# A fused attention and mixture-of-experts layer: accumulator rows load ahead of the last scatter, and the last stage works in five groups

## What is computed

```python
x = x + _layernorm(_L0_attn_ref(_layernorm(x), Wq, Wk, Wv, Wo))   # 16 heads of 16, causal, rotary
x = x + _layernorm(_L0_ffn_ref(_layernorm(x), gate_w, ...))
# _L0_ffn_ref: 16 experts (inner size 176), the 4 best of each row, and a shared expert (704)
combine = (one_hot(topk_idx, E) * topk_w[..., None]).sum(1)
shared = _silu_mul(x @ shared_gate_up.T, SI) @ shared_down.T * sigmoid(x @ shared_gate_vec.T)
def step(acc, ew):
    h = _silu_mul(x @ w_gu.T, I)
    return acc + h @ w_d.T * cw[:, None]
```

## Time and profile before

| | |
|---|---|
| timed runs, median of 3 | 605.13 us (604.32 to 607.23) |
| profiled execution, span | 615.7 us |
| PE, DVE, ACT, POOL busy | 519.5, 407.5, 342.5, 329.6 us |
| mean granted TensorE clock | 0.943 |
| DMA | 86.34 MB, mean 140 GB/s |

### The profile page before, as it was taken

The page is one execution under the profiler, slowest core; times in us unless marked ns, Lnnn a source line. Parts: engine busy times, 40 slices in busy tenths (PEclk is TensorE's granted clock), DMA queues, the critical chain, the costliest instruction groups (busy, mean ns, idle before and its releaser), DMA issues.

```text
span 615.7 us, 11608 instructions
## 1 busy us (share of the span) xinstructions
PE 519.5 (84%) x3550; PEld 399.0 (65%) x3550; DVE 407.5 (66%) x1005; ACT 342.5 (56%) x701; POOL 329.6 (54%) x357
## 2 busy tenths in 40 slices
PE   2738899899999998879778886989999999999473
PEld 1525455646565553457657775879888999999362
DVE  6528878888879766655815634747878666666237
ACT  2141476687578468756434315548777666666314
POOL 5331452482456124325476676707677887877624
PEclk9858899999999999979997997989999999999878
DMA  7241652445073440321046323568998988886594
GB/s 273 62 143 51 184 172 81 143 135 176 0 212 125 141 136 3 101 76 66 20 143 196 127 100 124 175 182 184 234 231 203 147 144 139 136 135 105 62 363 181
DMA packets 71034, 86.34 MB, mean 140 GB/s; under 512 B 6272, under 2 KB 64192, under 8 KB 70976
## 3 DMA queue, kind: packets, MB, share of 16 engines
q1 hardware_dynamic: 53264, 63.15, 32.9%
q0 software_dynamic: 14448, 19.31, 17.8%
q10 hardware_dynamic: 3264, 3.15, 1.5%
HBM read 33.68 MB, written 39.12 MB: 118 GB/s over the span
## 4 chain that ended last, share of the span: by engine, by line
PE 24%; DMA 10%; DVE 8%; issue 7%; ACT 3%; another core or an unknown queue 2%; POOL 1%; ACTq 0%; POOLq 0%; SPq 0%; DVEq 0%
PE gate_ps L1970 8%; DMA acc_dram<-yout,xin 7%; PE y_ps L1993 5%; PE y_ps L1944 2%; PE m_ps L1889 2%; PE up_ps L958 2%; PE gate_ps L958 2%; DMA added<-acc_dram 2%; DVE hid L1698 1%; DVE hid_lo L1724 1%; PE up_ps L1982 1%; PE up_ps L1981 1%; ACT hid_hi L1456 1%; DMA raw<-in_wex_dram 1%
## 5 line engine op out<-in xcount | busy, mean ns | idle before, releaser
L1386 POOL DMA_INDIRECT acc_dram<-yout,xin x79 | 126.5, 1602 | 53.8 <-ACT yout L1510 21.6
L715 DVE TENSOR_REDUCE nmax<-a_ps 128x2 f32<-128x768 f32 (+3 forms) x88 | 96.1, 1120 | 13.7 <-PE a_ps L857 13.2
L598 ACT ACTIVATE probs<-a_ps 128x1024 f32<-128x1024 f32 (+1 forms) x96 | 81.4, 883 | 28.1 <-PE a_ps L879 24.4
L497 POOL TENSOR_SCALAR_AFFINE_SELECT probs<-probs 128x256 f32<-128x256 f32 (+1 forms) x96 | 47.9, 508 | 90.1 <-ACT probs L598 89.9
L1374 POOL DMA_INDIRECT xs_dram<-xrow,idx x64 | 67.5, 1054 | 37.0 <-issue 24.2
L1970 PE MATMUL gate_ps<-w_all,rxT_hi 128*128 x316 | 78.5, 330 | 3.4 <-DVE rxT_lo L1747 2.0
L1772 DVE TENSOR_TENSOR h<-rsilu,gate_ps 128x176 f32<-128x176 f32 x79 | 26.6, 337 | 51.4 <-ACT rsilu L1495 38.5
L1993 PE MATMUL y_ps<-w_all,hT_hi 128*128 x237 | 57.1, 310 | 1.7 <-DVE hT_lo L1779 1.4
L1970 PEld LDWEIGHTS gate_ps<-w_all,rxT_hi 128*128 128x128 f32 x316 | 52.7, 190 | 5.0 <-issue 4.5
L852 PE MATMUL a_ps<-KTt,QT 96*128 96x128 bf16 (+3 forms) x256 | 50.5, 308 | 4.4 <-DVE nmax L715 2.2
L1970 PE MATMUL gate_ps<-w_all,rxT_lo 128*128 x158 | 51.5, 326 | 0.0
(11 more groups left out here) (315 smaller groups left out, 1376.7 us busy)
## 6 DMA issues: line engine op xcount, KB each, us to landing
xin<-xs_dram SPq DMA_DIRECT2D x79, 136.5 KB
xs_dram<-zeros SPq DMA_DIRECT2D x7, 1365.0 KB, 6.7
w_all<-in_wex_dram SPq DMA_DIRECT2D x16, 480.0 KB
QT<-parts SPq DMA_DIRECT2D x48, 128.0 KB
KTt<-parts SPq DMA_DIRECT2D x48, 128.0 KB
acc_dram<-zeros SPq DMA_DIRECT2D x6, 640.0 KB, 8.1
added<-acc_dram ACTq DMA_DIRECT2D x12, 256.0 KB, 10.1
x_all<-in_x_dram SPq DMA_DIRECT2D x4, 512.0 KB, 7.5
```

The costliest lines, as they stand in the source:

```text
L497: pool.affine_select(out=pr, in_=pr, pattern=[[0, nh], [1, P]], compare_op=ALU.is_ge, fill=0.0, base=0, channel_multiplier=-1).then_inc(ma ...
L598: nc.scalar.activation(dst, src, ACT.Exp, scale=float(DH) ** -0.5).then_inc(a_act, 1)
L715: nc.vector.tensor_reduce(nmax[:, i, h:h + nh].rearrange("p (b h) -> p b h", h=hb), src, AX.X, ALU.max, negate=True).then_inc(a_dve, 1)
L1386: pool.indirect_dma_start(out=acc[a][:, :], out_offset=bass.IndirectOffsetOnAxis(ap=xin[:, p % XIN, XROW - 1:XROW].bitcast(mybir.dt.uint32 ...
```

## The change

1. SP fetches the rows of tiles 0 to 8 (`EARLY`) while the last pages run, three loads of 128 rows a tile (`load_early`). The first follows the load of page 74, which waits for page 62 (`FINAL`), the last page with rows of `PARTS[0]`. They go into five places (`RING`): three `ring` buffers, the freed `raw0`, and the pair `before` and `spare`. Tiles 5 to 8 wait for a place (`kept_summed`).
2. DVE adds up tiles 0 to 5 between its page work (`add_first`, `add_second`) and takes the statistics of tiles 0 to 3 (`look`). Tables of steps say where. The sums of tiles 0 to 3 go into the unused halves of `m_ps` and `up_ps`.
3. Tiles 9 to 11 load when TensorE is through with the last page, tiles 12 to 15 an accumulator at a time when its last scatter has landed. SP issues all loads, ACT none.
4. TensorE adds up tiles 6 to 11, 13 and 15, DVE tiles 12 and 14. The end works in five groups, of 4, 4, 4, 2 and 2 tiles.
5. In the attention and in `late_norm` pairs of semaphores are merged into one; the waits are for the same instructions.

```diff
+FINAL = (PARTS[0].stop * P * K - E) // P + E - 1
+EARLY, RING, KEPT, HELD = 9, 5, 4, 6
+GROUPS = (slice(0, 4), slice(4, 8), slice(8, 12), slice(12, 14), slice(14, 16))
...
-        def by_pe(i):
-
-            return i % 2 == 1 or i // 2 in (1, 3, 5)
+        BY_PE = [6, 7, 8, 9, 10, 11, 13, 15]
+        PE_FULL = {6: 2, 7: 2, 8: 4, 9: 4, 10: 6, 11: 6, 13: 7, 15: 8}
...
+            def load_early(i):
+
+                for a in range(ACCS):
+                    sp.dma_start(fetched(i, a), acc[a][i * P:(i + 1) * P, :]).then_inc(early_in[i % RING], 16)
...
-            for i in range(ACCS):
-                sp.wait_ge(y_added[i], 16 * len(range(i, PAGES, ACCS)))
-            sp.wait_ge(r_y, PAGES)
-            for h in range(2 * B):
-                load_sums(sp, h, range(0, ACCS, 2 if h % 2 else 3))
...
+                if q == FINAL + XIN:
+                    load_early(0)
+                if FINAL + XIN <= q < FINAL + XIN + RING - 1:
+                    load_early(q - FINAL - XIN + 1)
+            for i in range(RING, EARLY):
+                sp.wait_ge(kept_summed, i - RING + 1)
+                load_early(i)
+
+            sp.wait_ge(r_down, PAGES)
...
+            for a in range(ACCS):
+                load_rest(a, slice(EARLY, PARTS[0].stop), rest_in)
+            for a in (1, 2, 0):
+                sp.wait_ge(y_added[a], 16 * len(range(a, PAGES, ACCS)))
+                for h in range(2):
+                    load_rest(a, GROUPS[3 + h], total_in[h])
...
+            def add_first(i):
+
+                dve.wait_ge(early_in[i % RING], 16 * ACCS * (i // RING + 1))
+                nc.vector.tensor_tensor(fetched(i, 0), fetched(i, 0), fetched(i, 1), ALU.add).then_inc(early_summed, 1)
+
+            def add_second(i):
+
+                dve.wait_ge(early_summed, i + 1)
+                nc.vector.tensor_tensor(summed(i), fetched(i, 0), fetched(i, 2), ALU.add).then_inc(kept_summed, 1)
...
+            ROWS_STEPS = {71: (add_second, 0), 72: (add_second, 1), 73: (look, 0), 74: (look, 1)}
+            HIDDEN_STEPS = {72: (add_second, 2), 73: (add_second, 3), 74: (look, 2), 75: (look, 3)}
+            FREE_STEPS = {68: (add_first, 0), 69: (add_first, 1), 71: (add_first, 2), 73: (add_first, 3),
+                          75: (add_first, 4), 77: (add_second, 4), 78: (add_first, 5), 79: (add_second, 5)}
...
+            for g in range(len(GROUPS) + 2):
+                if g < len(GROUPS):
+                    gathered(g)
+                if 0 <= g - 1 < len(GROUPS):
+                    shifted(g - 1)
+                if g >= 2:
+                    finish(g - 2)
...
+                if i == 10:
+                    pe.wait_ge(r_y, PAGES)
+                elif i == 15:
+                    pe.wait_ge(y_scaled, 1)
+                for a in range(ACCS):
+                    ins = nc.tensor.matmul(pe_places[n], ident[:], part_of(i, a), start=a == 0, stop=a == ACCS - 1,
+                                           skip_group_check=True)
+                ins.then_inc(pe_summed, 1)
```

More of the change, by code:

```diff
@@ L1231, in ffn_block, with fetched, kept, part_of @@
         block = ctx.enter_context(nc.Block())
-        sum_places = [ps[:, j, k * D:(k + 1) * D] for ps in (gate_ps, up_ps, m_ps) for j in range(2)
-                      for k in range(2)] + [y_ps[:, j, :] for j in range(TB)]
-        def by_pe(i):
-            return i % 2 == 1 or i // 2 in (1, 3, 5)
-        def summed(i):
[L1241 to L1250, removed]
+        def fetched(i, a):
+            c = i % RING
+            if c < RING - 1:
+                return ring[c][:, a, :]
+            return spare[:, a - 1, :] if a else before[:].rearrange("p a b -> p (a b)")
+        def kept(i):
+            return (m_ps, m_ps, up_ps, up_ps)[i][:, 1 - i % 2 if i < 2 else i % 2, D:2 * D]
+        BY_PE = [6, 7, 8, 9, 10, 11, 13, 15]
+        PE_FULL = {6: 2, 7: 2, 8: 4, 9: 4, 10: 6, 11: 6, 13: 7, 15: 8}
+        pe_places = [gate_ps[:, j, k * D:(k + 1) * D] for j in range(2) for k in range(2)] + [
+            y_ps[:, 0, :], y_ps[:, 1, :], y_ps[:, 2, :], up_ps[:, 0, 0:D]]
+        def summed(i):
+            if i < KEPT:
+                return kept(i)
+            if i < HELD:
+                return fetched(i, 0)
+            return pe_places[BY_PE.index(i)] if i in BY_PE else total[:, i, :]
+        def part_of(i, a):
+            if i < EARLY:
+                return fetched(i, a)
+            return added[:, a - 1, i, :] if a else total[:, i, :]
         @block.sync
@@ L1315, in _, with load_rest @@
                     expert(k)
-            for i in range(ACCS):
-                sp.wait_ge(y_added[i], 16 * len(range(i, PAGES, ACCS)))
-            sp.wait_ge(r_y, PAGES)
-            for h in range(2 * B):
-                load_sums(sp, h, range(0, ACCS, 2 if h % 2 else 3))
[L1322 to L1326, removed]
+                if q == FINAL + XIN:
[6 more added lines that the diff above has]
+            sp.wait_ge(r_down, PAGES)
+            def load_rest(a, tiles, landed):
+                to = added[:, a - 1] if a else total
+                sp.dma_start(to[:, tiles, :], acc[a][tiles.start * P:tiles.stop * P, :].rearrange(
+                    "(n p) d -> p n d", p=P)).then_inc(landed, 16)
+            for a in range(ACCS):
[4 more added lines that the diff above has]
+                    load_rest(a, GROUPS[3 + h], total_in[h])
+            for g, tiles in enumerate(GROUPS):
+                sp.wait_ge(y_out, g + 1)
+                sp.dma_start(out[:, tiles, :], total[:, tiles, :]).then_inc(out_stored, 16)
+            sp.wait_ge(out_stored, 16 * len(GROUPS))
         @block.gpsimd
@@ L1390, in _ @@
                     oob_is_err=True, compute_op=ALU.add).then_inc(y_added[a], 16)
-            for n in range(2 * B):
-                tiles = slice(n * TB // 2, (n + 1) * TB // 2)
-                root(n, y_var, mv[:, tiles, 1], y_eps, y_root, rs[:, tiles])
+            for g, tiles in enumerate(GROUPS):
+                root(g, y_var, mv[:, tiles, 1], y_eps, y_root, rs[:, tiles])
         @block.scalar
@@ L1778, in _ @@
                     dve.wait_ge(r_hhi, q + 1)
+                    beside(HIDDEN_STEPS.get(q))
                     nc.vector.tensor_tensor(hT_lo[:, q % 2], up_ps[:, q % 2, 0:D].rearrange("p (k n) -> p k n", k=2),
@@ L1788, in _, with gathered @@
                         expert_tail_low(k)
[L1791 to L1805 removed]
+                beside(FREE_STEPS.get(p))
+            def gathered(g):
+                tiles = GROUPS[g]
+                for i in range(max(tiles.start, KEPT), tiles.stop):
+                    if i in BY_PE:
+                        dve.wait_ge(pe_summed, PE_FULL[i])
+                    elif i >= HELD:
+                        dve.wait_ge(total_in[g - 3], 16 * ACCS)
+                        for a in range(1, ACCS):
+                            link(nc.vector.tensor_tensor(total[:, i, :], total[:, i, :], part_of(i, a), ALU.add))
+                    look(i)
+                dve.wait_ge(c_step, tiles.stop)
                 for i in range(tiles.start, tiles.stop):
```

110 lines of the change are left out of this document (48 added, 62 removed).

## The result

| | before | after |
|---|---|---|
| timed runs, median (range, runs) | 605.14 us (604.32 to 607.23, 4) | 598.13 us (594.58 to 600.61, 4) |
| after / before | | 0.9869 (0.9826 to 0.9912) |
| profiled execution, span | 615.7 us | 595.5 us (own time 597.27) |

The kernel became 7 us faster in this comparison. The forecast was 591 us with a range of 587 to 597 us, so the direction was right and the size was not: the median lies 1.1 us outside the range.

A forecast was written before the change was run, and what follows sets the result against it. TensorE was taken to bound the pages, then the last scatter's landing and the loads behind it the end. A gain of 15.8 us less 2.0 us of shift gave 605.13 - 13.8 = 591.3 us, said as 591, range 587 to 597 us.

The forecast's parts named there:

- T: The moment the last page's scatter-add into the accumulator has landed, 583.56 us before, forecast to move to 585.6 us.
- Term 2: Work added ahead of T, from DVE, the DMA engines and POOL: T moves by 1.1 + 0.7 + 0.2 = 2.0 us.
- The wait ... 1.5 us: At page 68 DVE waits for tile 0's early rows, 0 to 2.9 us, taken as 1.5; TensorE loses 1.1 us.
- From here I take 0.7 us on T: Early loads on busy DMA engines slow the scatters and move T by 0.7 us, between 0 and 8 us.
- T would not move: Alternative reading: engines take turns between queues, scatters keep half, so early loads cost T nothing, 0.7 us off the sum.
- Rival C: DVE's adds hold up POOL at nearly every scatter, 1 to 3 us more: 592 to 594 us; chance 0.04.
- Term 1: The end behind T shrinks from 32.1 to 16.3 us, since fewer loads wait there: 15.8 us gained.
- DVE at T + 5.9: Behind T, TensorE's cold adds of tiles 9 to 11 delay DVE, which reaches group 3 at about T + 5.9 us.
- B: Early loads saturate the DMA engines, scatters slip 8 us; 595 to 600 us, chance 0.14; sign: POOL waits 5 us or more.
- A: Complete cover: tile 0's rows land in time, TensorE's nine adds aren't late, end 14.5 us; 588 us, chance 0.17.
- D: Loads of pages 75 to 78 stand behind early loads on SP and starve TensorE: 608 us or more, chance 0.03.
- E: DVE's chain of five groups takes as long as the loads did and T slips: 602 to 608 us, chance 0.03.

The follow-up runs named there:

- e3: The changed kernel run again with no edit, beside the kernel before: 593.91 us, ratio 0.9815.
- e4: The changed kernel with DVE's first adds one to two pages later, so that the early rows are there: 593.48 us, ratio 0.9807.
- e11: The changed kernel run a third time with no edit: 594.85 us, ratio 0.9823.
- e1: The kernel before, run again with no edit: 605.70 us, ratio 1.0012.
- e9: The changed kernel with tiles 9 to 11 loaded one after the other, each with its own wait: 594.15 us, ratio 0.9823.
- e10: The changed kernel with both the later DVE steps of e4 and the loads by tile of e9: 592.87 us, ratio 0.9783.
- e6: The changed kernel with the loads of tiles 9 to 11 held until page 76's scatter has landed: 600.06 us, ratio 0.9913.

## Why the prediction came out as it did

**The mechanism was right.** The 24 loads behind T went away, the end shrank from 32.1 to 17.7 us, T moved by waits on the early rows and by a slower last scatter, and DVE waited for tile 0 at the place named. What failed are sizes: the wait for tile 0 (1.5 us forecast, 2.57 measured), the shift by the DMA engines (0.7, measured 1.3) and the end behind T (16.3, measured 17.7). Together they are the 2.9 us between 13.8 and 10.9 (62.35 - 51.40, from spans of 615.69 and 595.53 us). The other 4 us of the miss lie where the prediction had no term.

**Term 2, the shift of T: 2.0 us forecast, 3.5 us measured** (33.7 - 30.2).
- "The wait ... 1.5 us" was 2.23 + 0.34 us, and 3.08 us in e3. I took the middle between a lone store and a queue of loads. In after the three loads occupied SP 0.43 us each (issued at 542.60, 543.07 and 543.55 us), not 0.32, and the rows were usable 4.2 us behind the third issue. The step behind it, that 0.4 us are swallowed, held in each profile. So the loss was 2.2 instead of 1.1 us.
- "From here I take 0.7 us on T" was 1.3 us (5.17 - 3.85), and at another place. I looked for it in the backlog of POOL between 552 us and the last scatter; but from h(72) to the last `yout` it stays at 14.6 us, and from there to its scatter at 2.9. It came from the last scatter, beside the rest loads and those of accumulators 1 and 2. No run leaves these loads out, so their part in it is likely, by the table of durations below, and not shown. The backlog itself shows only in e4, where DVE doesn't wait: there no wait of DVE gives the scatters time to catch up.
- That "T would not move", as the prediction read the Trainium skill's rule of turns between queues ("DMA: Bandwidth & Descriptors", Queues, rings and completion order), isn't what the rows show: 6.08 us for page 77's scatter against 3.83. Whether the engines take turns no row here can tell.
- POOL delayed by DVE's adds, 0.2 us: the scatter that began at 568.85 us took 1.66 us instead of 1.54. Rival C is out.

**Term 1, the end behind T: 16.3 us forecast, 17.7 us measured.** In after it splits at the starts on DVE into 4.88 (577.83 to 582.71), group 3 3.19 (to 585.90), the `finish` of four tiles 1.18, group 4 1.96 (to 589.04), and 6.49 us. The forecast of 16.3 has 5.2 us up to group 3 and then 1.96 + 1.24 + 1.96 + 5.96, so the excess is in group 3 (1.2) and the last part (0.5), less 0.3 at the start:
- the loads took 4.5 us to land, not 3.1: the DMA share was still 1.10 in that stretch. They landed as DVE finished with group 2, so that "DVE at T + 5.9" didn't happen here. In e3 and e11 it did, at T + 6.3, and the excess is there: the rest loads landed 6.5 us behind the last page, and the nine adds took 5.6 us.
- group 3 took 1.2 us longer, because TensorE adds up tile 13 and was cold: idle 1.96 us, clock 0.52 from 582.3 to 585.3 us, six records in 2.89 us against 1.40 us for tile 9. I had put the cold clock on tiles 9 to 11, where the idle time of 2.59 us ahead left the granted clock at 1.00. In e3, with 2.68 us idle, tile 9 took 2.93 us. Which of the groups falls into the cold is not the same in each execution.
- the nine adds themselves took 4.2 us where I said 4.1, and that is luck: two errors cancel. An f32 matmul leaves two records, so the six records in 2.72 us in the earlier trace rows are three matmuls, one tile. Nine cold ones would be 8.2 us; e4, cold but for its last records, shows 7.2.
- the last part took 0.5 us more: "the same POOL root" has a `finish` of four tiles beside it now, not two (below).

**The rivals.** The first median, 598.13 us, lies in B's range of 595 to 600 us, but B is not what happened. POOL's waits for landed scatters, its sign, are 4.6 us between 535 and 578 us in after; from 540 to 575 us e1 has 4.0 us without any early load, e3 4.3 us and e11 1.8 us with them. The longest in after, 2.1 us, ends at 551.86 us, 0.76 us behind the end of its `yout`, which DVE's wait had made late; an undisturbed scatter starts 0.77 us behind (557.12). B's mechanism is seen in e4 alone. A needed rows in time. D: no page load was waited for by TensorE. E: the end behind T fell from 32.1 to 17.7 us.

**Beyond the terms.** With the sizes of the runs the sum is 605.1 - 10.9 = 594.2 us, which is what e3 and e11 gave (593.9, 594.9), inside the range. The other 4 us of the first comparison are in pages 0 to 68 of its profiled execution. That the other three timed runs behind its median had the same is likely and not shown. They lie in pages 12 to 32, 1.7 us of them beside a fallen clock; what starts it stays open. The profile of before was itself long in the part ahead of these pages. The range made no room for such a difference between two comparisons.

## What to carry to other kernels

When loads move ahead of a wait, ask when the first of them can be issued and how long one takes at a DMA share near 1, and put the first user behind that; here it was 5 to 6 us from the first issue to the first use, not 2. A second path can end as late as the one that is shortened (here last page, rest loads, TensorE's adds; in e3 and e11 it was the later one), so both must be brought forward together: e4 alone gave nothing, e9 alone nothing that is measurable, both together the lowest time (e10, not yet clear of the noise). And count from a mark that the change doesn't touch, in more than one profile of each kernel, before a few us of a difference are believed.

## What the runs showed of the hardware

- A POOL instruction on a tiny tile waited for a DVE add with two SBUF operands that ran at the same time. `yrs` (128x2) starts at 589.12 us and takes 1.17 us, to 590.29, and the `finish` add runs from 589.00 to 590.22 us. On 128x4 the same instruction takes 0.23 us at 574.27 us, where no such add runs, and 1.18 us at 581.70 beside one. In e1, with an add of two tiles (0.69 us), the chain has the row below. The Trainium skill ("SBUF — State Buffer", Who interferes with whom) has it so, the later one blocks; the rows agree.

```profile
598.88 0.64 POOL yrs L1342
```

- Scatter-adds took longer beside plain loads. From start to landing: 3.83 us at a DMA share of 0.57 and of 0.59 (before), 4.21 us at 0.63 (e4, page 78), 3.85 us at 0.87 (after, 538.37 us); but 6.08 us at 1.02 (after, page 77), 5.62 us at 1.13 (e10), 6.14 us at 1.08 (e9), 6.66 us at 0.95 (e6).
- TensorE after an idle time of 2.59 us was at full clock in after, at half clock after 1.96 us in the same execution, and at half clock after 2.68 us in e3. The length of the idle time just ahead didn't decide it alone.
